# Sums over pieces: all high-part matmuls of a row first, then all low-part ones

## What is computed

```python
for i in range(3):                                    # L0
    h = h + segment_sum(h[src], dst)
    h = relu(bn(h @ W1[i] + b1[i])); h = relu(bn(h @ W2[i] + b2[i]))
# L1: messages weighted by a sigmoid of source and target scores, summed, GRU
for w in conv_w:                                      # L2, five steps
    h = gru(segment_sum((h @ w)[src], dst), h)
out = x + segment_sum(relu(layernorm(x))[src], dst) @ W.T + b   # L3
```

## Time and profile before

| | |
|---|---|
| median of 3 runs | 4018.3 us (4017.14 to 4019.05) |
| profiled execution | 4019.86 us, its span 4017.6 us |
| TensorE matmuls busy | 3710.6 us, 92% of the span |
| TensorE weight loads busy | 2906.7 us, 72% |
| VectorE busy | 2909.2 us, 72% |
| ScalarE busy | 2512.6 us, 63% |
| GpSimd busy | 304.7 us, 8% |
| mean granted TensorE clock | 0.994 of full speed |

### The profile page before, as it was taken

One profiled execution on the slowest core, in us unless ns is written; L12 is line 12 of the kernel. 1 busy time (PEld: TensorE's weight loads), 2 busy tenths in 40 slices (PEclk: granted clock), 3 DMA queues, 4 the chain that ended last, 5 costly groups with the idle time before them and its releaser, 6 DMA issues.

```text
span 4017.6 us, 57803 instructions
## 1 busy us (share of the span) xinstructions
PE 3710.6 (92%) x16970; PEld 2906.7 (72%) x16970; DVE 2909.2 (72%) x6934; ACT 2512.6 (63%) x4580; POOL 304.7 (8%) x658
## 2 busy tenths in 40 slices
PE   0148889999999999999899999999999999999999
PEld 0126678888888545555688888888888888888887
DVE  9999956656667788887676766666666676677755
ACT  1039856666666787777566556655655655666665
POOL 0011100000023110000330000000000000033300
PEclk9999999999999999999899999999999999999999
DMA  3039954555544332221254444444444444434444
GB/s 65 0 138 366 366 162 136 159 139 141 159 132 121 100 82 72 72 63 47 77 140 118 126 138 127 117 137 135 120 133 136 120 119 137 125 102 116 118 135 136
DMA packets 361521, 515.39 MB, mean 128 GB/s; under 512 B 159908, under 2 KB 228253, under 8 KB 360824
## 3 DMA queue, kind: packets, MB, share of 16 engines
q1 hardware_dynamic: 340572, 458.67, 40.4%
q0 software_dynamic: 7696, 46.93, 3.2%
q10 hardware_dynamic: 12938, 6.05, 0.7%
HBM read 396.98 MB, written 43.87 MB: 110 GB/s over the span
## 4 chain that ended last, share of the span: by engine, by line
PE 49%; POOL 1%; ACT 1%; DVE 1%; issue 0%; DMA 0%; SPq 0%; ACTq 0%; POOLq 0%; DVEq 0%
PE ps L2270 40%; PE ps L2382 3%; PE ps L2383 3%; PE ps L2385 1%; PE ps L2384 1%; ACT wide L2108 0%; PE ps L2367 0%; PE ps L2308 0%; PE ps L2302 0%; PE ps L2411 0%; PE ps L2406 0%; POOL inv L2179 0%; PE ps L2293 0%; PE ps L2285 0%; POOL root L2178 0%
## 5 line engine op out<-in xcount | busy, mean ns | idle before, releaser
L2270 PE MATMUL ps<-wide,hi 128*128 128x512 f32 (+2 forms) x5537 | 2149.7, 391 | 12.3 <-DVE lo L2604 7.7
L2270 PE MATMUL ps<-wide,lo 128*128 128x512 f32 (+2 forms) x5537 | 2075.7, 379 | 0.0
L2108 DVE CAST wide<-ring 128x1024 fp32r<-128x1024 uint8 (+1 forms) x1274 | 1001.7, 786 | 617.3 <-PE ps L2270 610.9
L2108 ACT CAST wide<-ring 128x1024 fp32r<-128x1024 uint8 (+1 forms) x1274 | 1237.0, 971 | 3.0 <-DMA ring<-count 2.3
L2270 PEld LDWEIGHTS ps<-wide,hi 128*128 128x128 f32 x5537 | 1041.9, 188 | 212.9 <-issue 18.5
L2270 PEld LDWEIGHTS ps<-wide,lo 128*128 128x128 f32 x5537 | 1043.0, 188 | 190.3
L2465 ACT CAST hi<-high 128x128 fp32r<-128x128 f32 x1274 | 380.8, 299 | 922.3 <-PE ps L2270 517.0
L2266 PE MATMUL ps<-hN,hB 128*128 128x512 f32 (+1 forms) x1274 | 522.9, 568 | 3.0 <-DVE aggT L2428 1.7
L2458 ACT ACTIVATE hN<-aggT,source_scores 128x512 f32<-128x512 f32 (+1 forms) x637 | 427.7, 694 | 115.0 <-PE ps L2266 83.6
L2586 DVE TENSOR_TENSOR hN<-hN,ring 128x512 f32<-128x512 f32 (+1 forms) x637 | 400.8, 666 | 101.6 <-ACT hN L2458 96.1
L2266 PEld LDWEIGHTS ps<-hN,hB 128*128 128x128 f32 x1274 | 241.0, 190 | 262.1 <-issue 208.2
(11 more groups left out here) (246 smaller groups left out, 3333.8 us busy)
## 6 DMA issues: line engine op xcount, KB each, us to landing
ring<-count SPq DMA_DIRECT2D x490, 320.0 KB, 3.0
ring<-count SPq DMA_DIRECT2D x441, 256.0 KB, 2.7
ring<-count SPq DMA_DIRECT2D x490, 224.0 KB, 2.6
wide<-aggT POOLq DMA_DIRECT2D x49, 896.0 KB, 6.5
count<-aggT SPq DMA_DIRECT2D x49, 800.0 KB, 4.0
hB<-mid SPq DMA_DIRECT2D x192, 32.0 KB, 1.9
hN<-mid SPq DMA_DIRECT2D x192, 32.0 KB, 1.9
hB<-squares SPq DMA_DIRECT2D x96, 32.0 KB, 2.0
```

The lines of the kernel that those rows point to most:

```text
L2108: return copy(wide[:, g % WIDE_SLOTS, c0:c1].rearrange("p (t u f) -> p t u f", u=2, f=P), rows[:, g % row_slots, c0:c1].rearrange("p (t f ...
L2270: ins = e.matmul(ps[:, c, 0:size], part[:, g % CUT_SLOTS, :], wide[:, g % WIDE_SLOTS, w0:w0 + size], start=k == 0 and part is hi, stop=k = ...
```

## The change

In each row TensorE now goes through all pieces with `hi` and then through all pieces with `lo`. The wait for `lo` stands between the two passes. `summed` is raised by the lo matmul of each bank in the last row, as before, and `used` by the last of the row. The weighing rows stay as they were.

```diff
                         else:
                             e.wait_ge(s["hi"], g + 1)
-                            e.wait_ge(s["lo"], g + 1)
                             e.wait_ge(s["wide_act"], g + 1)
...
-                            for part in () if weighing else (hi, lo):
-                                ins = e.matmul(ps[:, c, 0:size], part[:, g % CUT_SLOTS, :], wide[:, g % WIDE_SLOTS, w0:w0 + size],
-                                               start=k == 0 and part is hi, stop=k == NB - 1 and part is lo,
-                                               skip_group_check=True)
-                            if not weighing and k == NB - 1 and c + 1 < len(SUMS[q]):
+                            else:
+                                e.matmul(ps[:, c, 0:size], hi[:, g % CUT_SLOTS, :], wide[:, g % WIDE_SLOTS, w0:w0 + size],
+                                         start=k == 0, stop=False, skip_group_check=True)
+                        if not weighing:
+                            e.wait_ge(s["lo"], g + 1)
+                        for c, (w0, size) in enumerate(() if weighing else SUMS[q]):
+                            ins = e.matmul(ps[:, c, 0:size], lo[:, g % CUT_SLOTS, :], wide[:, g % WIDE_SLOTS, w0:w0 + size],
+                                           start=False, stop=k == NB - 1, skip_group_check=True)
+                            if k == NB - 1 and c + 1 < len(SUMS[q]):
                                 ins.then_inc(s["summed"], 1)
```

## The result

The changed kernel takes 4034.97 us (median of 6 runs, 4033.37 to 4036.72), the kernel before 4018.32 us (6 runs, 4017.14 to 4020.55): ratio 1.0040, 95% interval 1.0029 to 1.0051. So it is slower by 16.7 us between the medians, where the forecast said 12.1 (4030.4 us) with its own range up to 4035. A second comparison gave 4034.11 against 4019.47 us, ratio 1.0036 (1.0022 to 1.0049), 14.6 us. The two profiled executions lie 13.5 us apart (4033.37 and 4019.86 us).

The account below looks back on a forecast made before the run. TensorE, busy 92% of the span, bounds the kernel as a chain of matmuls. Ends 11.7 plus very end 0.5 minus lo wait 0.1 gave +12.1 us: 4030.4 us, own range 4027 to 4035, 8 in 10 from 4014 to 4044.

Parts of the forecast that it names:

- The spacing of full pieces: Starts of neighbouring 512-column matmuls in the two flows: nothing changes, from 229.6 against 229.2 ns.
- the rival of cheap repeated weights: TensorE spends up to 2.8 ns less between equal-weight matmuls, gaining up to 24 us, so 4006 us; chance 12%.
- the estimate made from the Trainium skill: About 216 ns per isolated 512-column gap, 13 ns on 8,526 matmuls: over 100 us lower; the prediction rejected it.
- The ends of thirds: Where one third hands banks to the next: later release and faster asking make TensorE wait for takes, 11.7 us in sum.
- the first stall: Second flow, end 1 to 2: TensorE waits for bank 0's take, going on at 2.28 us instead of 1.83.
- a second one for bank 2 and its refill: Second flow, end 1 to 2: hi for bank 2 at 2.88 instead of 2.82 us, plus 0.08 refill.
- Neighbours: Spacing of successive matmuls in the flows under changed bank and repeated weights: taken as 0, ends +20 and -24 us.
- a cost of changing the bank: Rival: each bank change costs 3.6 ns, as seen after 256-column pieces; +20 us, 4050 us; chance 10%.
- The wait for lo: TensorE's wait for lo moves behind the hi pass: gain 0.1 us, ends 0 and 0.3.
- The very end: Last row before the output matmuls: bank 0 ready later, output matmuls and stores 0.5 us later.

Follow-up runs that it names:

- e9: Full change plus equal pieces (third 0 five of about 486 columns, third 2 except the very last four of 448): 4042.53 us, kernel before 4019.69.
- e10: Full change with third 0's first piece widened from 384 to 512 columns, summing 128 unused columns: 4072.20 us, kernel before 4019.69.
- e1: New order in rows 1 to 47 of every third, old order in its first and last row: 4025.96 us, kernel before 4020.62.
- e2: Old order in rows 1 to 47 of every third, new order in its first and last row: 4027.92 us, kernel before 4020.62.
- e5: Kernel before with the new order only in the last row of each third: 4023.79 us, kernel before 4019.47.
- e6: Kernel before with the new order only in the first row of each third: 4025.02 us, kernel before 4019.47.
- e7: Kernel before, old order, but second-flow thirds 2 and the thirds 0 behind them start on a free bank: 4014.51 us, kernel before 4019.47.
- e3: Full change, but in rows 1 to 47 the short piece comes last in the hi pass and first in the lo pass: 4032.65 us, kernel before 4020.62.
- the repeat: The full change timed once more, unaltered, beside the kernel before on another chip: 4034.11 us against 4019.47, ratio 1.0036.

## Why the prediction was right, and where a term was wrong

*The spacing of full pieces* was right, from 229.6 against 229.2 ns: neither the change of bank nor equal weights in a row cost or give anything. Third 1's middles, 107.27 us in both orders, show it, and the two don't merely cancel: all eight distances of such a row have the median 227 ns in either order, with the bank changed or kept and the weights repeated or not. e9 shows the same for undisturbed rows of 486 columns, and e10 for a row of ten full pieces. So the rival of cheap repeated weights is out: every matmul still had its own 188 ns load beside the matmul before it, and equal weights were worth nothing. With it goes the estimate made from the Trainium skill ("TensorE: Matmul & The Clock Gate", "Back-to-back issue gap"): 512 columns start 226.7 ns apart here, not 216, with the granted clock at 0.995 of full speed in the mean. What the Trainium skill says there ("Step-by-step: what each phase is for") of loading once and multiplying often, no run here shows, as this kernel loads before every matmul, no matter how they are ordered.

*The ends of thirds* were the right mechanism. e1 takes them away, e2 leaves only them, e5 and e6 split them, e7 removes the wait without touching the order. In the first flow the reckoned 6.4 us measured 6.0. In the second 5.3 measured 3.2: the first stall came out exactly (2.28 us), but I had added a second one for bank 2 and its refill (0.06 + 0.08), and in the trace there is only one. That makes about 1.7 of the 2.1 us too much; the rest is 2 to 0, reckoned at 0.19 us an end and measured at 0.09.

*The middles* are the term that was mis-sized: "Neighbours ... I take 0" should have been 5 us. The difference of 114.3 and 117.9 ns for the 256-column kinds was in the text, but as the upper end of a cost of changing the bank, which it isn't: in the new order, where all change bank, the 256-column matmuls of the second flow have a median distance of 114 ns in both passes. It goes with the place of a short matmul among full ones. Means over pairs had also mixed what stands where in a row. By place, third 0's distances in the old order are 171, 175, 236, 228, 233, 231 and four times 227 ns (medians of the second flow): the four full matmuls behind the short pair are slowed too. The new order parts the pair and has 174 or 175, 231, 231, 236, 227 or 228 in each pass. At 0.443 ns a column an undisturbed row's 2,432 columns, swept twice, would take 2156 ns; with one such place it takes 2180, with two 2191 (the sums of medians lie some ns higher). e3 brings most undisturbed rows back to 2180 by joining the pair again, in one bank. With no unequal piece (e9, e10, third 1) the order makes no difference to an undisturbed row.

*The wait for lo* gave nothing instead of 0.1 us: ScalarE's share of `wide` is ready no earlier.

*The very end*: the first output matmul starts 1.99 us after the last row's start instead of 1.62, 0.4 us against the reckoned 0.5, but from the last row to the end of the span it is 13.8 against 13.7 us in the two traces, 14.8 in the repeat and 15.2 in e1, which has the old order there. That stretch ends with the stores, and it varies by more than the 0.5 us, which so can't be told.

Sum of the rows: 9.1 + 5.1 = 14.2 us (9.1 + 5.3 in the repeat), against 16.7 and 14.6 measured. Some of the nearness of the total is luck: the ends were put 2.6 us too high and the middles 5.1 us too low, two errors of opposite sign, and the first comparison lies at the very upper edge of the prediction's own range.

**What stays open** is why a matmul of fewer than 512 columns disturbs its followers, whether the bank has a part in it, why 486 and 448 columns run above the rate of 512, and what picks one of two paces for the same row. The runs show where it costs, not by what.

## What to carry to other kernels

Where banks are handed over, look at both sides of the handover: how long before the end the first bank is complete, and how fast the next user asks for banks. An order that finishes all banks together and asks for all at once pays on both sides. A free bank to start on takes a wait away: with one, this kernel gained 5 us in its old order. That it would also pay for the new order is likely and not shown. And measure the distance of matmuls by their place in the row, not as a mean over kinds: here 9 ns a row, a third of the whole change, didn't show in the mean of full pieces. And compare rows of several thirds before calling a small difference an effect: the same row can settle at two paces some 30 ns apart.

## What the runs showed of the hardware

Among its like, an FP32R matmul of 512 columns takes 226.7 ns from start to start whatever the bank, the weights or the order; behind the shorter ones of third 0 it takes up to 236. Two matmuls of 384 columns side by side in one bank are cheaper than two apart, by 11 ns in an undisturbed row of ten. The same row of eight matmuls of 448 columns takes 1.62 us in one third and 1.65 in another of the same execution (e9). Five equal pieces of 486 columns take 2206 ns a row where 384 and four times 512, the same 2,432 columns, take 2180. And repeated loads of the same weights are all carried out, 188 ns each, beside the matmul before them.
